# Relation passes of a four-layer graph network: 22 of 806 row gathers replaced by single-row copies issued from SyncE and ScalarE

## The reference, cut to what matters

```python
def _rgcn_layer(x, W, SW, b, src, dst, rel):
    xt = jnp.einsum('nd,rde->rne', x, W)          # 8 relations: one table of rows for each
    msg = xt[rel, src]                            # one row of 128 for each edge
    agg = jax.ops.segment_sum(msg, dst, num_segments=x.shape[0])
    return jax.nn.relu(agg + x @ SW + b)
x = _rgcn_layer(entity_emb, w1, sl1, b1, src, dst, edge_type)
x = _rgcn_layer(x, w2, sl2, b2, src, dst, edge_type)
```

## Time and profile before

| | |
|---|---|
| median of three runs | 5118.82 us (5105.4 to 5121.59) |
| the profiled execution's own time | 5124.63 us |
| its span, first to last instruction | 5123.3 us |
| busy over the span | PE 2855.5, DVE 1971.1, ACT 677.7, POOL 2395.5 us |
| first relation pass, first gather to last matmul | 2747.4 to 3896.2 us |
| second relation pass | about 3948 to 5097 us |

### The profile page before, as it was taken

How to read it: one execution, slowest core, us unless ns; L and a number is a source line. 1 busy time by engine, 2 the same in 40 slices (tenths; PEclk the granted TensorE clock), 3 DMA queues, 4 the chain that set the end, 5 groups by cost and what they waited for, 6 DMA issues and landing times.

```text
span 5123.3 us, 41736 instructions
## 1 busy us (share of the span) xinstructions
PE 2855.5 (56%) x12033; PEld 2017.8 (39%) x12033; DVE 1971.1 (38%) x3965; ACT 677.7 (13%) x1897; POOL 2395.5 (47%) x2466
## 2 busy tenths in 40 slices
PE   4666889946666656656626444444346444444343
PEld 3555445534444444444523333333333333333333
DVE  7676765655555555555562111111112111111111
ACT  2334010012222222222311000000001000000000
POOL 3000000055545555555313666666663666666665
PEclk8787989967777777777757555555557555555555
DMA  3444735444333443343304111111114111111111
GB/s 117 201 190 209 306 151 224 188 126 118 109 110 107 118 112 109 114 114 109 85 2 132 47 47 45 46 46 47 46 48 127 46 47 46 47 48 46 46 46 49
DMA packets 294311, 508.93 MB, mean 99 GB/s; under 512 B 68232, under 2 KB 239610, under 8 KB 288968
## 3 DMA queue, kind: packets, MB, share of 16 engines
q1 hardware_dynamic: 216304, 344.29, 18.9%
q0 software_dynamic: 77792, 161.98, 11.4%
HBM read 389.30 MB, written 116.74 MB: 99 GB/s over the span
## 4 chain that ended last, share of the span: by engine, by line
PE 37%; another core or an unknown queue 23%; issue 20%; DVE 6%; POOL 5%; ACT 5%; DMA 2%; ACTq 0%; DVEq 0%; SPq 0%; POOLq 0%
PE sums L587 9%; PE sums L748 8%; POOL edge_buffers L559 5%; PE sums L1105 3%; PE sums L1163 3%; PE sums L1108 3%; ACT trio L1185 3%; PE sums L670 3%; DVE edge_buffers L570 2%; PE sums L1119 2%; PE sums L666 2%; DMA edge_buffers<-rel_t,relidx 2%; PE sums L1477 2%; ACT adj_window L697 1%
## 5 line engine op out<-in xcount | busy, mean ns | idle before, releaser
L559 POOL DMA_INDIRECT edge_buffers<-rel_t,relidx x1612 | 1530.0, 949 | 888.1 <-issue 368.4
L587 PE MATMUL sums<-edge_buffers 128*128 128x128 f32 x3224 | 963.4, 432 | 1332.2 <-issue 1000.8
L587 PEld LDWEIGHTS sums<-edge_buffers 128*128 128x128 f32 x3224 | 748.0, 308 | 1548.9 <-issue 1547.3
L1061 POOL DMA_INDIRECT round_buffers<-xs_t,srcs x806 | 801.5, 994 | 1008.0 <-DVE round_buffers L1240 454.2
L570 DVE TENSOR_SCALAR edge_buffers<-iota,rel 128x128 f32<-128x128 f32 x1612 | 335.5, 300 | 1961.0 <-remote 1506.3
L1163 PE MATMUL sums<-round_buffers 128*128 128x128 f32 x1612 | 282.1, 321 | 441.5 <-ACT trio L1185 363.7
L1163 PEld LDWEIGHTS sums<-round_buffers 128*128 128x128 f32 x1612 | 236.1, 221 | 475.1 <-ACT trio L1185 390.5
L748 PE MATMUL sums<-adj_chunk,H 128*128 128x448 f32 x1050 | 400.2, 542 | 15.6 <-issue 14.4
L1231 DVE TENSOR_TENSOR positive<-positive,sums 128x384 f32<-128x384 f32 x310 | 154.2, 497 | 539.4 <-ACT positive L1175 504.8
L1108 PEld LDWEIGHTS sums<-round_buffers 128*128 128x128 f32 x1612 | 298.0, 238 | 99.5 <-issue 84.2
L1105 PE MATMUL sums<-round_buffers,ident 128*128 128x408 f32 x620 | 317.0, 601 | 28.9 <-DVE trio L1292 24.9
(11 more groups left out here) (273 smaller groups left out, 2683.4 us busy)
## 6 DMA issues: line engine op xcount, KB each, us to landing
adj_chunk<-adj SPq DMA_DIRECT2D x19, 5600.0 KB, 15.9
adj<-adj_window SPq DMA_DIRECT2D x21, 3850.0 KB, 11.2
round_buffers<-xd_t SPq DMA_DIRECT2D x806, 68.0 KB
round_buffers<-rel_tile SPq DMA_DIRECT2D x62, 832.0 KB
edge_buffers<-rel_t,relidx POOLq DMA_INDIRECT x1612
rel_t<-edge_buffers SPq DMA_DIRECT2D x50, 512.0 KB, 3.8
round_buffers<-xs_t,srcs POOLq DMA_INDIRECT x806
round_flags<-seg_tile SPq DMA_DIRECT2D x62, 26.0 KB
```

The costliest lines, as they stand in the source:

```text
L559: nc.gpsimd.indirect_dma_start(slot(t), None, table[:, :], bass.IndirectOffsetOnAxis(ap=index[:, t:t + 1], axis=0)).then_inc(slot_sem(t), 16)
L587: nc.tensor.matmul(sums[:, bass.ds(place[k], P)], slot(t), round_hots(i)[:, k, :], start=False, stop=False).then_inc(summed_n, 1)
L1061: nc.gpsimd.indirect_dma_start(rows[r % RING][:, k * RW:(k + 1) * RW], None, xs_t[:, :], bass.IndirectOffsetOnAxis(ap=srcs[:, t:t + 1], ax ...
```

## The change

Of the 806 tiles of a pass, ten are taken from POOL and given to SP (tiles 78, 157, ... every 79th), and twelve to ACT (tiles 65, 131, ... every 66th). For such a tile the engine loads the 128 row numbers into registers, 16 at a time (eight loads), and issues 128 DMAs of one row of 512 bytes, each from the place in `rel_t` that a register holds, into one of two slots per engine of a new buffer `rows_by_hand`. It may begin a tile when PE has summed the last but one that it fetched. POOL gathers the other 784 into the same ring of 26, now counted by its own tiles. PE and DVE do the same work as before; PE waits on other semaphores for the 22 tiles. The row numbers (`fetchidx`) come from two small inputs that SP loads ahead of the attention rounds and that one DVE instruction turns into `type * NP + src`.

```diff
+FETCHED = 12
+BY_SP = list(range(78, ET - 10, 79))
+BY_ACT = list(range(65, ET - 10, 66))
+BY_POOL = [t for t in range(ET) if t not in BY_SP and t not in BY_ACT]
+RINGED = 2 * U
...
             def gather_rows_of_tiles():
                 nc.gpsimd.wait_ge(*tabled)
                 nc.gpsimd.wait_ge(*ready)
-                for t in range(ET):
-                    nc.gpsimd.wait_ge(summed_n, summed0 + max(0, t - 2 * U + 1))
+                for p, t in enumerate(BY_POOL):
+                    nc.gpsimd.wait_ge(summed_n, summed0 + (BY_POOL[p - RINGED] + 1 if p >= RINGED else 0))
                     nc.gpsimd.indirect_dma_start(
-                        slot(t), None, table[:, :],
-                        bass.IndirectOffsetOnAxis(ap=index[:, t:t + 1], axis=0)).then_inc(slot_sem(t), 16)
+                        ring_slot(p), None, table[:, :],
+                        bass.IndirectOffsetOnAxis(ap=index[:, t:t + 1], axis=0)).then_inc(ring_sem(p), 16)
+
+            def fetch_rows(eng, engine, who, tiles):
+                for j, t in enumerate(tiles):
+                    if j > 1:
+                        eng.wait_ge(summed_n, summed0 + tiles[j - 2] + 1)
+                    for lo in range(0, P, 16):
+                        at = nc.values_load_multi_w_load_instructions(
+                            fetchidx[who:who + 1, j, lo:lo + 16], engines=(engine,), min_val=0, max_val=R * NP - 1,
+                            skip_runtime_bounds_check_because="a node's row in one of the relations' tables")[1]
+                        for k in range(16):
+                            eng.dma_start(fetched_slot(who, j)[lo + k:lo + k + 1, :],
+                                          table[bass.ds(at[k], 1), :]).then_inc(s_fetched[who][j % 2], 16)
...
+                        if t in by_hand:
+                            who, j = by_hand[t]
+                            got = fetched_slot(who, j)
+                            nc.tensor.wait_ge(s_fetched[who][j % 2], fetched_count(who, j))
+                        else:
+                            p = ringed[t]
+                            got = ring_slot(p)
+                            nc.tensor.wait_ge(ring_sem(p), got0[ring_sem(p)] + 16 * (p // RINGED + 1))
...
             gather_rows_of_tiles()
+            fetch_rows_on_sp()
+            fetch_rows_on_act()
             compare_rounds()
             add_tiles()
...
         def feed_rounds():
+            nc.sync.wait_ge(*tabled)
+            s_fetch.did(nc.sync.dma_start(fetchidx, a["fetch_src"]))
+            s_fetch.did(nc.sync.dma_start(fetchtype, a["fetch_type"]))
...
+            V.did(V.after(s_fetch.now()).scalar_tensor_tensor(out=fetchidx, in0=fetchtype, scalar=float(NP), in1=fetchidx,
+                                                              op0=ALU.mult, op1=ALU.add))
```

More of the change, by code:

```diff
@@ L37 @@
 CH = NP // NCH
+FETCHED = 12
[3 more added lines that the diff above has]
+RINGED = 2 * U
+assert len(BY_SP) <= FETCHED and len(BY_ACT) <= FETCHED and not set(BY_SP) & set(BY_ACT)
+assert len(BY_SP) % 2 == 0 and len(BY_ACT) % 2 == 0
 EPS = 1e-5
@@ L529, in build, with ring_slot, ring_sem, fetched_slot @@
         s_tab = Dma(sem("s_tab"))
[L531 to L535, removed]
+        ringed = {t: p for p, t in enumerate(BY_POOL)}
+        by_hand = {**{t: (0, j) for j, t in enumerate(BY_SP)}, **{t: (1, j) for j, t in enumerate(BY_ACT)}}
+        s_fetched = [[sem(f"s_rows_by_{n}{k}") for k in (0, 1)] for n in ("sp", "act")]
+        fetched_before = [0, 0]
+        def ring_slot(p):
+            return (rows if p % RINGED < U else win)[:, p % U, :]
+        def ring_sem(p):
+            return (s_row if p % RINGED < U else s_odd)[p % U]
+        def fetched_slot(who, j):
+            return fetched[:, 2 * who + j % 2, :]
+        def fetched_count(who, j):
+            return 16 * P * (fetched_before[who] + j // 2 + 1)
         def round_hots(i):
@@ L556, in gather_rows_of_tiles, with fetch_rows_on_sp, fetch_rows_on_act @@
                 nc.gpsimd.wait_ge(*ready)
-                for t in range(ET):
-                    nc.gpsimd.wait_ge(summed_n, summed0 + max(0, t - 2 * U + 1))
+                for p, t in enumerate(BY_POOL):
+                    nc.gpsimd.wait_ge(summed_n, summed0 + (BY_POOL[p - RINGED] + 1 if p >= RINGED else 0))
                     nc.gpsimd.indirect_dma_start(
-                        slot(t), None, table[:, :],
-                        bass.IndirectOffsetOnAxis(ap=index[:, t:t + 1], axis=0)).then_inc(slot_sem(t), 16)
+                        ring_slot(p), None, table[:, :],
[11 more added lines that the diff above has]
+                                          table[bass.ds(at[k], 1), :]).then_inc(s_fetched[who][j % 2], 16)
+            def fetch_rows_on_sp():
+                nc.sync.wait_ge(*ready)
+                for s in s_rt[1:]:
+                    nc.sync.wait_ge(*s.now())
+                nc.sync.wait_ge(summed_n, summed0)
+                fetch_rows(nc.sync, ENG.SP, 0, BY_SP)
+            def fetch_rows_on_act():
+                nc.scalar.wait_ge(*indexed)
+                nc.scalar.wait_ge(*ready)
+                for s in s_rt[1:]:
+                    nc.scalar.wait_ge(*s.now())
+                nc.scalar.wait_ge(summed_n, summed0)
+                fetch_rows(nc.scalar, ENG.Activation, 1, BY_ACT)
             def compare_rounds():
@@ L585, in add_tiles @@
                         t = i * U + k
-                        nc.tensor.wait_ge(slot_sem(t), got0[slot_sem(t)] + 16 * (t // (2 * U) + 1))
-                        nc.tensor.matmul(sums[:, bass.ds(place[k], P)], slot(t), round_hots(i)[:, k, :],
+                        if t in by_hand:
[6 more added lines that the diff above has]
+                            nc.tensor.wait_ge(ring_sem(p), got0[ring_sem(p)] + 16 * (p // RINGED + 1))
+                        nc.tensor.matmul(sums[:, bass.ds(place[k], P)], got, round_hots(i)[:, k, :],
                                          start=False, stop=False).then_inc(summed_n, 1)
@@ L597, in sum_in_banks @@
             cnt[summed_n] += ET
-            for s in (*s_row, *s_odd):
-                cnt[s] += 16 * (IT // 2)
+            for p in range(len(BY_POOL)):
+                cnt[ring_sem(p)] += 16
+            fetched_before[0] += len(BY_SP) // 2
+            fetched_before[1] += len(BY_ACT) // 2
             return closed
@@ L1462, in build @@
         buffers = sb("edge_buffers", [P, 4, U, P])
+        fetched = sb("rows_by_hand", [P, 4, P])
         rows, hot, win, pbc = (buffers[:, j] for j in range(4))
@@ L1496, in build @@
         ready = relation_tables(s_par.now(), columns_turned)
+        indexed = V.now()
         wused = T.now()
         nc.sync.wait_ge(*wused)
+        nc.sync.wait_ge(*indexed)
         w2 = s_par.did(nc.sync.dma_start(wrel[:, :, :], a["L3_gnn_w2"].rearrange("r d e -> d r e")))
@@ L1542 @@
     pieces = np.stack([dst[::P], dst[P - 1::P]], axis=1).reshape(PIECES)
+    by_hand = [(v + v)[:FETCHED] for v in (BY_SP, BY_ACT)]
     arrays = {
+        "fetch_src": src.reshape(ET, P)[by_hand], "fetch_type": typ.reshape(ET, P)[by_hand],
         "src_col": src.reshape(ET, P).T, "type_col": typ.reshape(ET, P).T, "dst_col": dst.reshape(ET, P).T,
```

3 lines of the change are left out of this document (added).

## The result

The change takes 5701.45 us (median of four runs, 5673.84 to 5712.87) against 5120.2 us of the kernel before: ratio 1.1123, 95% interval [1.1101, 1.1145]. I had forecast 5066 us. What happened is the rival "rows are slow beside gathers" (chance 0.28, 5817 us).

The account below looks back on a forecast made before the run. POOL's gathers were taken as the longest stream, with 136 us a pass of waits for PE. 5124.6 - 55 (gathers removed) + 2 (DVE instruction) = 5071.6 us profiled, 5066 us median; own range 5035 to 5100, overall range 5035 to 5450.

Parts of the forecast that it names:

- rows are slow beside gathers: Rival for the passes: rows take 1.64 us while POOL gathers, PE and POOL stop, 5817 us; chance 0.28.
- the price of a row: SP's and ACT's row DMAs in the passes: 0.50 us each, chosen between bounds of 0.50 and 1.64 us.
- the 1.52 us of round 2, and the 1.64 of round 20: SP's slower copies in the attention rounds, 19.79 / 13 and 9.86 / 6 us; 1.64 was taken as upper bound.
- The "Against": Objection to 0.50 us a row: PE does nothing in round 0 but works in a pass; busy DMA alone isn't the cause.
- Gathers removed: POOL's gathers in the passes: 22 fewer a pass save 27.5 to 31.2 us, over two passes 55 (at most 62).
- Register loads: SP's and ACT's queues: eight loads of row numbers for each tile, 1.19 us each.
- The limits of 0.64 and 0.78 us a row: Highest row prices at which tiles stay hidden: 0.64 us on ACT, 0.78 us on SP.
- The rival that came true: Slow rows, chance 0.28: 43 rows go beside 80 us of gathers, 85 while POOL stops; period 122.5, pass 1491 us.
- Shared issue: Rival: SP and ACT share what issues a DMA, 0.667 us a row where both issue; 5077 to 5155 us, chance 0.10.
- PE paces the pass: Rival: PE, not POOL, sets the pass, so each gather saved becomes a longer slot wait; 5119 us, chance 0.08.
- PE's slow stretches put the 136 us on top: Passes of the kernel before: POOL's gathers are the longest stream, and PE's slow stretches add 136 us of slot waits.
- DMAs lengthen POOL's gathers: Rival in the passes: rows lengthen gathers, 24 us over 5,632 rows; 5090 us, chance 0.04.

Follow-up runs that it names:

- e7: Changed kernel with PE's float32 matmul of each tile replaced by a one-column float16 matmul, nothing summed: 6044.28 us (before 5096.7).
- e4: Changed kernel without POOL's gathers behind the first 26 of a pass, sums not the reference's: 4335.91 us (before 5096.6).
- e15: Changed kernel with a POOL pause of some 2.5 us behind each fourth gather: 5723.82 us (before 5100.82).
- e5: Changed kernel with the 22 tiles' rows fetched by nobody, two whole-block DMAs per engine and pass instead: 5035.25 us, ratio 0.9883 to the kernel before.
- e1: Changed kernel with only ACT fetching its twelve tiles, SP's ten given back to POOL: 5645.72 us, ratio 1.1078 to the kernel before.
- e9: Changed kernel with four tiles on SP and six on ACT, their rows fetched by nobody: 5073.05 us, ratio 0.9946 to the kernel before.
- e16: Kernel before with a POOL pause of some 2.5 us behind each eighth gather: 5328.1 us (before unaltered 5100.82).
- e3: Changed kernel with fewer tiles, four a pass on SP and six on ACT: 5099.67 us, ratio 1.0005 to the kernel before.
- e6: Changed kernel with two neighbouring rows per DMA, 64 DMAs a tile instead of 128: 5081.25 us, ratio 0.9966 to the kernel before.
- e10: Changed kernel with 16 neighbouring rows per DMA, 8 DMAs a tile: 5045.29 us, ratio 0.9889 to the kernel before.
- e17: Kernel before with one POOL fill of some 0.8 us behind each eighth gather: 5124.39 us, ratio 1.0009 to it unaltered.
- e11: Changed kernel with a POOL pause of some 2.5 us behind each fourth gather, on chip 9: 5274.97 us (before 4391.67 there).
- e18: Changed kernel with one POOL fill of some 0.8 us behind each eighth gather: 5690.36 us, ratio 1.112 to the kernel before.
- e13: Kernel before with one POOL fill of some 0.8 us behind each eighth gather, on chip 9: 4524.07 us, ratio 1.0306 to it unaltered.

## Why the prediction was wrong, step by step

**The step that failed** is the price of a row, "I choose 0.50: in round 1 POOL gathers without a pause as in the passes, and SP alone issues beside it". Over the passes a row cost 1.23 us (ACT) and 1.51 (SP) beside gathers, and 4.3 where they go on unbroken for over 20 us. Round 1 is 6.47 us long, and it isn't like a pass, as the trace of the kernel before shows. I wrote "with gathers at 0.94 us beside it", but the gather of 0.94 us in the earlier trace rows begins at 1056.40, behind the copies, which end at 1054.65. Behind the one of 3.22 us stand:

```profile
1050.64 1.57 POOL L1061 DMA_INDIRECT round_buffers<-xs_t,srcs  x1 [0.30 <-issue]
1052.51 1.88 POOL L1061 DMA_INDIRECT round_buffers<-xs_t,srcs  x1 [0.30 <-issue]
1054.69 1.41 POOL L1061 DMA_INDIRECT round_buffers<-xs_t,srcs  x1 [0.30 <-issue]
```

These gathers begin 1.9 to 3.5 us apart, against 1.25 in a pass. The price of a row beside gathers 1.25 us apart could be read in round 2, where POOL's last gather begins at 1090.97. SP's copies in 1079.7:1095, then in 1096:1099.3:

```profile
1079.74 15.48 SPq L1076 DMA_DIRECT2D round_buffers<-xd_t  x5
...
1096.11 3.42 SPq L1076 DMA_DIRECT2D round_buffers<-xd_t  x7
```

The first five take 16.2 us to the start of the sixth, 3.2 us each, and these seven 0.49 us each. So the 1.52 us of round 2, and the 1.64 of round 20, were means over a slow stretch and a quick one, and no upper bound. That 1.64 came near the mean of the passes is luck. The "Against" was wrong too: PE's and ACT's work were not what made the copies slow (e7 for PE; and in 2846:2864 of the change PE stands and ACT computes nothing while the rows are slow). e4 and e15 show the cause by taking away the gathers or the way in which they follow each other.

**What was right.** Gathers removed: 55 to 62 us forecast, 60 to 61.5 measured (e5, the added DVE instruction and index loads included, whose 2 us can't be told apart). Register loads at 1.19 us: 1.29 (ACT) and 1.22 us. The limits of 0.64 and 0.78 us a row: exceeded, and PE waited.

**The rival that came true** was sized at 1.64 us a row. Its own formula with the measured prices, which include the register loads, gives 80 / 1.23 = 65 rows beside gathers and 63 x 0.59 = 37 us for the others, a period of 117 us; measured 119 from tile to tile, and 1453 and 1443 us a pass against 1491. Its mechanism, PE at ACT's tile, POOL's ring full, the rest quick, is what the timelines show.

**The other rivals.** Shared issue: refuted by e1 and e4. PE paces the pass: refuted by e5 and e9, where each gather removed shortens the pass by its 1.4 us. But the sentence "PE's slow stretches put the 136 us on top" stopped half way: those stretches are caused by POOL's gathering (e16). DMAs lengthen POOL's gathers: they don't (953 ns against 949), and yet DMAs by hand take about 0.012 us each (0.008 to 0.016) from the pass by POOL's longer waits, a term that the sum put at nothing. At 5,632 DMAs that is an estimated 68 us (45 to 90), as much as the 62 saved: had all rows been hidden, the change would probably still have gained nothing. I had given a cost of each DMA 0.04, with 0.01 us a row as the point from which it decides; e3 lies about there. How a DMA of another engine lengthens POOL's waits wasn't shown; that it delays PE's steps is an argument only.

By the Trainium skill's "DMA: Bandwidth & Descriptors", section "Rules for kernel authors", small transfers should be coalesced. e6 and e10 agree: the price followed the number of DMAs, and 16 rows in each brought the time to within 10 us of fetching nothing.

**What stays open.** What slows the steps. That the gathers do it is shown; what in them isn't. Beside a break in the gathering, their mean rate would fit: 8 in some 12.4 us with the pauses of e16 (quick), 8 in 10.7 us with those of e17 (slow), 8 in 10 us unbroken (slow), and in round 1 of the attention layer POOL never stopped for more than 0.31 us while gathers 1.9 to 3.5 us apart left the copies quick. Nor does it end at once: in round 2 the copies stay slow until 1095.94, 4 us behind the end of the last gather. No run has the same mean rate with and without breaks. Nor is it known why one chip doesn't show it; each chip was used on one occasion, so the two can't be told apart. The change itself wasn't run there, and e11's rows of 0.43 to 0.49 us were taken with the pauses in.

## What to carry to other kernels

Take the price of an operation from a stretch at least as long and as steady as the one in which it will stand, and look at its rate over time instead of one short sample: here the first 5 us said 0.6 us a row and the same stretch 20 us later 4.3. A mean over a slow and a quick part is no bound either: look at the single starts. Before a second engine is loaded with work, set the queue's own steps (register moves, address steps) beside their undisturbed duration; where a 29 ns move takes 700 ns, each DMA issued there costs many times what it seems to. Where an engine waits in short, regular gaps, ask whether the gaps are what lets the others run, and try a kernel on more than one chip before tuning to such an effect.

## What was unexpected of the hardware

- Beside indirect DMAs that GpSimd issues 1.25 us apart without a break, steps of SP's and ACT's queues come to last 0.70 us (29 to 37 ns for a move or an address step and 213 to 225 ns for a DMA otherwise): 0.42 of the moves between 5 and 10 us, all from 20 us on. Filled pauses of 2.4 us behind every fourth gather prevent it (e15), one of 0.7 us behind every eighth doesn't (e18).
- PE is slowed too: 163 steps of 2.1 to 3 us between matmuls of the passes in the kernel before, 6 with 2.4 us behind every eighth gather (e16).
- One chip of six showed hardly any of it: PE has 3 such steps in e13 and 109 in e17, the same program, and the kernel before takes 4391.67 us there, against 5,097 to 5,122 on the others.
- A DMA's price in an issuing queue hardly depended on 0.5 or 1 KB: 213 and 243 ns an instruction, 1.23 and 1.31 us from start to start on ACT beside gathers.
